# Two Swin blocks in fp16 halves: P transposed by DMA instead of by TensorE

## What is computed

```python
# per block; windows of 8 x 8 points after a shift by 4; 12 heads of 16
xn   = layernorm(x)
q,k,v = split(window(roll(xn)) @ w_qkv + b_qkv)
attn = softmax(q @ k.T * 16**-0.5 (+ rel_bias + shift_mask in the first block))
x    = x + unroll(unwindow((attn @ v) @ w_proj + b_proj))
x    = x + gelu(layernorm(x) @ w_fc1 + b_fc1) @ w_fc2 + b_fc2
```

## Time and profile before

| | before |
|---|---|
| median of 3 runs | 4314.11 us (4303.97 to 4317.73) |
| profiled execution, its span | 4314.22 us, 4312.3 us |
| TensorE matmuls, busy | 4027.5 us, 93% |
| VectorE | 3364.9 us, 78% |
| GpSimd | 3062.7 us, 71% |
| ScalarE | 2709.6 us, 63% |
| packets of the DMA queue, share of 16 engines | 54.9% |
| granted TensorE clock, mean | 0.999 |

### The profile page before, as it was taken

The page is one execution under the profiler, slowest core; times in us unless marked ns, Lnnn a source line. Parts: engine busy times, 40 slices in busy tenths (PEclk is TensorE's granted clock), DMA queues, the critical chain, the costliest instruction groups (busy, mean ns, idle before and its releaser), DMA issues. The chain is left out here.

```text
span 4312.3 us, 175439 instructions
## 1 busy us (share of the span) xinstructions
PE 4027.5 (93%) x66384; PEld 2912.2 (68%) x66384; DVE 3364.9 (78%) x9085; ACT 2709.6 (63%) x5921; POOL 3062.7 (71%) x6257
## 2 busy tenths in 40 slices
PE   4999999999999999999999999999999999999998
PEld 2666667667766666776676677667667766766665
DVE  6887777778778777787777778787777778777785
ACT  1666666666666666666666666666666666666665
POOL 4777777777777777777777777777777777777664
PEclk9999999999999999999999999999999999999999
DMA  4655556556565655555555555556555655565553
GB/s 98 104 96 100 98 95 99 102 95 99 104 98 97 100 102 92 103 100 96 98 100 98 97 99 102 97 97 101 102 91 101 100 97 98 100 101 96 90 95 61
DMA packets 1544449, 420.50 MB, mean 98 GB/s; under 512 B 1441334, under 2 KB 1542074, under 8 KB 1543612
## 3 DMA queue, kind: packets, MB, share of 16 engines
q1 hardware_dynamic: 1543612, 409.29, 54.9%
HBM read 31.56 MB, written 25.17 MB: 13 GB/s over the span
## 5 line engine op out<-in xcount | busy, mean ns | idle before, releaser
L573 PE MATMUL ps_s<-xh,w_fc 128*128 128x512 f16 x3840 | 909.7, 380 | 60.7 <-ACT stage L687 47.6
L941 DVE TENSOR_TENSOR hid<-scaled,hid 128x512 f16<-128x512 f32 x768 | 597.9, 779 | 449.7 <-POOL hid L1109 430.7
L1047 POOL TENSOR_TENSOR rstd<-vare,half 128x2 f32<-128x2 f32 x520 | 361.2, 695 | 801.5 <-DVE vare L881 801.5
L586 PE MATMUL bank<-w_fc,hid 128*128 128x192 f16 x9216 | 847.7, 246 | 77.7 <-DVE hid L941 71.9
L586 PEld LDWEIGHTS bank<-w_fc,hid 128*128 128x128 f16 x9216 | 764.6, 98 | 156.7 <-DVE v_blk L897 80.6
L573 PEld LDWEIGHTS ps_s<-xh,w_fc 128*128 128x128 f16 x3840 | 335.3, 97 | 621.0 <-ACT scaled L701 217.5
L1109 POOL TENSOR_SCALAR hid<-scaled 128x512 f16<-128x512 f32 x768 | 609.4, 794 | 182.8 <-ACT scaled L701 182.2
L701 ACT ACTIVATE scaled<-ps_s,b_fc 128x512 f32<-128x512 f32 x768 | 529.3, 690 | 308.9 <-DVE hid L941 306.8
L693 ACT ACTIVATE pt<-ps_t 128x768 f16<-128x768 f32 x512 | 415.3, 811 | 324.0 <-PE ps_t L530 316.8
L666 ACT ACTIVATE xs<-xn 128x192 f16<-128x192 f32 x512 | 184.6, 361 | 579.0 <-POOL xn L1053 579.0
L449 PE MATMUL bank<-w_qkv,xh 128*128 128x384 f16 x2560 | 500.9, 326 | 6.2 <-DMA xh<-xs 3.6
(11 more groups left out here) (113 smaller groups left out, 7341.9 us busy)
## 6 DMA issues: line engine op xcount, KB each, us to landing
x_img<-in_x_dram SPq DMA_DIRECT2D x256, 96.0 KB, 2.2
out_dram<-y_img SPq DMA_DIRECT2D x256, 96.0 KB, 1.9
xh<-xs SPq DMA_TRANSPOSE x520, 2.8
qkt<-qk SPq DMA_TRANSPOSE x512, 4.0
ot<-os SPq DMA_TRANSPOSE x512, 2.3
stage<-in_L_conv_fc_w_dram SPq DMA_DIRECT2D x2, 384.0 KB, 4.3
stage<-in_L_conv_w_fc_dram SPq DMA_DIRECT2D x2, 384.0 KB, 4.0
stage<-in_L_conv_qkv_w_dram SPq DMA_DIRECT2D x2, 288.0 KB
```

What stands on the lines that cost most here:

```text
L573: last = mm(ps_s[:, u % 2, :].rearrange("p (a t) -> p a t", a=GROUP), w_fc1[layer][:, part, m * 128:(m + 1) * 128], xh[:, p % 2 * GROUP:(p ...
L586: mm(bank[:, 0:C], hid16[:, hs, m, tok], w_fc2[layer][:, ws, m, :], start=(m == 0 and i == 0), stop=False)
L941: v.tensor_tensor(hid16[:, 1, m, :], hid[:, u % 2, :], hid16[:, 0, m, :], ALU.subtract)\
```

## The change

P is not transposed by TensorE any more. ScalarE makes the high half of P straight from `p_tok`, in the slot of the exponential, and VectorE the low half; both halves lie in `p16`, and one DMA transposition of 12 blocks (`p_turn`) brings them into `pt`. The banks `ps_t` become `ps_h` and hold the MLP's hidden products and outputs. `projection` goes into `ps_o` instead of `ps_qk`. The written order changes with it.

```diff
-        ps_t = ctx.enter_context(nc.psum_tensor("ps_t", [128, 2, 512], F32))
+        ps_h = ctx.enter_context(nc.psum_tensor("ps_h", [128, 2, 512], F32))
+        p16 = stage[:, 1, 0:2, :].rearrange("p r n -> p (r n)").bitcast(F16).rearrange("p (r s n) -> p r s n", r=2, s=2)
@@ SyncE
+                def p_turn(n):
+                    ge("p_lo", n)
+                    ge("pv", n - 2)
+                    sp.dma_start_transpose(pt[:, n % 2].rearrange("p s g t -> p (s g) t"),
+                                           p16[:, n % 2].rearrange("p s n -> p (s n)"))\
+                        .then_inc(LANDED["pt_in"][n % 4], 16)
+                if live(s):
+                    p_turn(s)
                 if live(s + 2):
                     qk_turn(s + 2)
@@ TensorE
-                def p_transpose(n):
...
                 def pv_product(n):
-                    if mlp and place == 3:
-                        ge("resid2", p * GROUP + 1)
-                    else:
-                        ge("o_norm", n - 1)
+                    ge("resid1", n - 2)
                     ge("v_lo", n)
-                    ge("p_lo", n)
+                    landed(pe, "pt_in", n)
...
                 def projection(n):
-                    if live(n + 5):
-                        ge("qk_lo", n + 5)
-                    else:
-                        ge("resid1", n - 1)
+                    ge("o_norm", min(n + 1, ENDS))
                     landed(pe, "ot_in", n)
...
                 def hidden(m):
-                        ge("exp_done", min(s, ENDS))
                     if m >= 2:
                         ge("gelu", u - 2)
+                    else:
+                        ge("resid2", (p - 1) * GROUP + 2 + m)
...
                     scores(s)
-                if live(s - 3):
-                    projection(s - 3)
-                if live(s - 1):
-                    p_transpose(s - 1)
+                if live(s + 3):
+                    qk_product(s + 3)
...
                 if live(s):
                     shift_scores(s)
-                if live(s + 3):
-                    qk_product(s + 3)
+                if live(s - 3):
+                    projection(s - 3)
                 if mlp and place == 0:
-                    for m in range(3):
+                    for m in range(4):
                         hidden(m)
@@ ScalarE
                 def p_hi(n):
-                    ge("tp", n)
-                    copy(pt[:, n % 2, 0].rearrange("p (b g) t -> p b (g t)", b=2), ps_t[:, :, 0:3 * TOK], ACT.Copy)\
+                    ge("exp_done", n)
+                    landed(act, "pt_in", n - 2)
+                    copy(p16[:, n % 2, 0], p_tok[:, n % 2].rearrange("p g a k -> p (g a k)"), ACT.Copy)\
...
-                if live(s - 1):
-                    p_hi(s - 1)
                 if live(s):
                     exp(s)
+                    p_hi(s)
@@ VectorE
-                    v.tensor_tensor(pt[:, n % 2, 1].rearrange("p (b g) t -> p b (g t)", b=2), ps_t[:, :, 0:3 * TOK],
-                                    pt[:, n % 2, 0].rearrange("p (b g) t -> p b (g t)", b=2), ALU.subtract)\
+                    v.tensor_tensor(p16[:, n % 2, 1], p_tok[:, n % 2].rearrange("p g a k -> p (g a k)"), p16[:, n % 2, 0],
+                                    ALU.subtract).then_inc(S["p_lo"], 1)
...
-                if mlp and place == 2:
-                    mlp_residual(p * GROUP + 1, ps_o)
                 if live(s + 5) or live(s - 3):
                     centre(s + 5)
-                if live(s - 1):
-                    p_lo(s - 1)
+                if mlp and place == 2:
+                    mlp_residual(p * GROUP + 1)
                 if mlp and place == 0:
                     hidden_lo(0)
+                if live(s):
+                    p_lo(s)
```

More of the change, by code:

```diff
@@ L227, in swin_program @@
             "centred rstd bn1a bn1 ln1 hi1 lo1 qk_mm v_mm mask_set qk_hi qk_lo v_hi v_lo "
-            "s_mm max_done shift exp_done tp p_hi p_lo pv inv_done o_norm o_hi o_lo "
+            "s_mm max_done shift exp_done p_hi p_lo pv inv_done o_norm o_hi o_lo "
             "pr resid1 bn2a bn2 ln2 hi2 lo2 fc2 resid2".split(), TOTAL)
@@ L234, in swin_program @@
         S = {name: sem(name) for name in COUNT}
-        LANDED = {name: [sem(f"{name}{r}") for r in range(4)] for name in ("xh_in", "ot_in", "qkt_in")}
+        LANDED = {name: [sem(f"{name}{r}") for r in range(4)] for name in ("xh_in", "ot_in", "qkt_in", "pt_in")}
         x_loaded = [sem(f"x_loaded{h}") for h in range(2 * SLABS)]
@@ L474, in v_product @@
                     _, layer, t = visit(n)
-                    if place == 1 or p < 0 or p == 0 == place:
-                        ge("v_lo", n - 1)
-                    else:
-                        ge("resid2", p * GROUP + (-1, None, 0, 2)[place])
+                    ge("v_lo", n - 1)
                     for w in range(2):
@@ L490, in rel_scores @@
                     _, layer, t = visit(n)
-                    if place == 1:
-                        ge("gelu", p * HC + HC - 1)
                     ge("exp_done", n - 1)
@@ L576, in hidden, with mlp_out @@
                     last.then_inc(S["fc1"], 1)
-                def mlp_out(n, bank):
+                def mlp_out(n):
                     _, layer, t = visit(n)
+                    bank = ps_h[:, n % 2]
                     tok = slice((t % GROUP) * TOK, (t % GROUP + 1) * TOK)
@@ L605, in slot @@
                     x_transpose(s + 6)
-                if live(s) and place != 1:
+                if live(s):
                     rel_scores(s)
@@ L630, in slot @@
                     shift_scores(s)
-                if live(s + 3):
-                    qk_product(s + 3)
+                if live(s - 3):
+                    projection(s - 3)
                 if mlp and place == 0:
-                    for m in range(3):
+                    for m in range(4):
                         hidden(m)
-                if mlp and place == 2 and visit(p * GROUP)[1] == 1:
-                    y_transpose(p * GROUP + 1)
+                if mlp and place == 2:
+                    mlp_out(p * GROUP + 1)
+                    if visit(p * GROUP)[1] == 1:
+                        y_transpose(p * GROUP + 1)
                 if mlp and place > 0:
-                    ge("v_lo", min(s, ENDS))
-                    if s > ENDS:
-                        ge("resid2", p * GROUP + (0, -1, 0, 2)[place])
-                    mlp_out(p * GROUP + (0, 0, 2, 3)[place], ps_v)
-                if mlp and place == 0:
-                    hidden(3)
+                    mlp_out(p * GROUP + (0, 0, 2, 3)[place])
             tr_reader = ["x_in", -1]
@@ L686, in exp @@
                     ge("shift", n)
+                    ge("p_lo", n - 2)
                     nc.scalar.activation(p_tok[:, n % 2].rearrange("p g a k -> p a g k"),
@@ L980, in slot @@
                 if mlp and place > 0:
-                    mlp_residual(p * GROUP + (0, 0, 2, 3)[place], ps_v)
+                    mlp_residual(p * GROUP + (0, 0, 2, 3)[place])
                 if live(s + 6):
```

38 lines of the change are left out of this document (13 added, 25 removed).

## The result

| | time (median) | ratio to before, 95% interval |
|---|---|---|
| before | 4315.15 us (4303.97 to 4317.73, 4 runs) | 1 |
| changed | 5000.89 us (4982.45 to 5009.01, 4 runs) | 1.1586 (1.1557 to 1.1615) |

The kernel is slower by 686 us. I had forecast 4875 us, 560 us slower, with a range up to 5040.

The account below looks back on a forecast made before the run. VectorE was taken as a second bound beside TensorE, with a VectorE-GpSimd chain in place 0. Places summed to 4.04 us, plus 0.33 for `p_lo`: 4.37 per phase, times 128 is 560, 4314 + 560 = 4874, said 4875; range 4700 to 5040.

Parts of the forecast that it names:

- forecast's own upper end: The highest total of the forecast's own sum, without rivals: 5.1 us per phase, giving 4965 us.
- late transposition: Rival: P's DMA transposition lands after 7.3 us, `pv_product` in place 0 is 1.3 us late, 5040 us; chance 0.10.
- round trip: VectorE's residual waits for row maximum, subtraction on TensorE and projection: 2.04 us against 0.88, 1.16 more per slot.
- Place 0: First slot of a phase: 1.16 us of VectorE waiting plus 0.88 for `p_lo` in the chain, 2.04 us longer.
- Place 1: Second slot of a phase: output product waits for a later last `hidden_lo`; +1.16 and about +0.95 by block, mean +1.05 us.
- TensorE's work behind it is unchanged: +1.16: Place 1, first block: after the first output product's wait TensorE's work stays the same, so the slot grows 1.16 us.
- Places 2 and 3: Last two slots of a phase: place 2 mean -0.05 us without the transposes, place 3 mean +1.0 from VectorE's list.
- y transposition: Place 2, second block: it stands between the two output products and waits for the first one's residual, about +0.2 us.
- `p_lo` from SBUF: VectorE's `p_lo` with both inputs in SBUF: +0.13 us each in two and a half slots, +0.33 per phase.
- The transposition is hidden: P's DMA transposition lands about 9 us behind its row maximum, `pv_product` comes at about +11: hidden by some 2 us.
- below any time considered here: The DMA queue's packets, with 6144 blocks more, take 3540 to 3720 us together, less than any time considered.
- The price of the transposes: TensorE's six transposes per visit take 0.66 us, 338 us in all, gained only where TensorE is waited for.

Follow-up runs that it names:

- Experiment 4: Changed kernel with 24 extra small matmuls on TensorE in place 1, in the wait for the last `hidden_lo`: 4887.4 us, ratio 1.1323.
- experiment 2: Changed kernel with `p_lo` put ahead of the first `hidden_lo` in place 0 again: 4993.7 us, ratio 1.1578.
- experiment 5: Both orders put back in the changed kernel, plus the projection back in `ps_qk` with TensorE's order and waits of before: 4502.7 us, ratio 1.0435.
- experiment 7: The kernel before with P's six TensorE transposes done twice: 4531.75 us, ratio 1.0506.
- Experiments 1: Changed kernel with the projection ahead of `qk_product` and the subtraction of the maximum again on TensorE, still into `ps_o`: 4838.9 us, ratio 1.1208.
- 3: Changed kernel with both the projection's order on TensorE and `p_lo`'s order in place 0 put back: 4718.1 us, ratio 1.0943.
- 8: The kernel before with one more, unread DMA transposition of 12 blocks per visit, issued ahead of `qk_turn`: 4370.7 us, ratio 1.0137.
- 12: Experiment 5 with only P's high half transposed (6 blocks instead of 12) from the third visit on: 4437.6 us, ratio 1.0284.
- 9: Experiment 5 with `qk_turn` issued behind `o_turn` in SyncE's list: 4845.5 us, ratio 1.1233.

## Why the prediction was right, and what it missed

The direction, the mechanism and nearly all slot lengths came out as forecast; the time lies 126 us above the forecast. It is also above the forecast's own upper end of 4965. That the stated range holds it is luck: its upper end, 5040, was the time of the late transposition, a rival that did not happen. The forecast's own range was also added up too narrowly: a round trip of 1.0 to 1.3 us counted in three places, with `p_lo` at 0 to 1.1, gives 3.6 to 5.6 us per phase, some 4770 to 5030 us, and not 3.8 to 5.1.

In mean slot lengths the profiled run (4982 us) grew by 2.47, 1.96, -0.07 and 0.85 us in places 0 to 3, 5.21 us per phase. The sum had 2.04, 1.05, -0.05 and 1.0, and 0.33 for `p_lo`, 4.37 us; 0.84 x 128 is the 107 us by which this run is over the forecast.

- *The round trip.* Forecast 2.04 us against 0.88, in every slot; the trace has 2.04, 2.03 (2447.82 less 2445.79) and 2.09 (2456.81 less 2454.72), in 512 slots, 588 us of waiting against "some 500". Right.
- *Place 0.* Forecast 14.6; median 14.68, mean 15.0. The second `hidden_lo` is 2.36 us later, forecast 2.04. The median is right, but of the 2.36 only 2.04 was priced; the rest is the first `hidden_lo`, 1.02 us long instead of 0.69. The mean is 0.3 us higher for another reason that I had no term for: in 26 of 126 phases the granted clock falls to 0.50 in this place, and these are 16.2 us long on average, the others 14.7.
- *Place 1: the term that was mis-sized.* "TensorE's work behind it is unchanged: +1.16" holds in block 1, 6.81 to 7.92, +1.11. In block 2, where I forecast +0.95, the median went from 6.32 to 8.90, +2.58. The wait before the output product rose to 2.2 us as forecast, but I priced the work behind it at its old duration. In 51 of 62 phases of block 2, and in 22 of 64 of block 1, the granted clock halves after this wait, and 18 matmuls take 3.06 us instead of 1.66. Experiment 4 isolates it: 113 us. In means place 1 grew by 1.96 us instead of 1.05, and 0.91 x 128 is 116 us. The other misses nearly cancel: place 0 took 0.43 us more, place 3 took 0.15 less, and the 0.33 for `p_lo` did not come.
- *Places 2 and 3.* Forecast 7.4 and 6.9. Mean of both blocks 7.58 and 6.8. Right within 0.2; the second block's extra (8.01 against 7.13) is larger than the 0.2 that I gave the y transposition.
- *`p_lo` from SBUF.* Forecast +0.13 us each; it takes 950 ns against 956 before:

```profile
L890 DVE TENSOR_TENSOR stage<-stage 128x768 f16<-128x768 f32 x512 | 486.4, 950 | 6.2 <-ACT stage L676 5.4
```

  The 0.33 us of this term came elsewhere, in the first `hidden_lo` (0.69 to 1.02 us), which now runs beside GpSimd's second `hidden_hi`. That the sum has the right amount there is luck. Beside `p_lo` it is GpSimd that pays, `rstd` 695 to 972 ns:

```profile
L1028 POOL TENSOR_TENSOR rstd<-vare,half 128x2 f32<-128x2 f32 x520 | 505.5, 972 | 1214.3 <-DVE vare L863 1214.3
```

```profile
2450.26 0.95 DVE L890 TENSOR_TENSOR stage<-stage 128x768 f16<-128x768 f32 x1
...
2450.49 1.27 POOL L1028 TENSOR_TENSOR rstd<-vare,half 128x2 f32<-128x2 f32 x1 [3.27 <-DVE vare L863]
...
2458.89 0.70 POOL L1028 TENSOR_TENSOR rstd<-vare,half 128x2 f32<-128x2 f32 x1 [2.48 <-DVE vare L863]
```

  The first `rstd` began 0.23 us into a `p_lo` and took 1.27 us. The second began 0.16 us ahead of the next `p_lo` (2459.05) and took 0.70. The Trainium skill (SBUF — State Buffer, section "SBUF: two separate sides") says that of a VectorE instruction with two SBUF inputs and a GpSimd one that reads SBUF, the one that starts first gets the shared ports for the whole instruction and the other is blocked. The first `rstd` agrees with it in direction. The second pair does not: this `p_lo` began 0.54 us ahead of `rstd`'s end and still took 0.95 us. In the changed kernel `rstd` of place 0 ends ahead of `p_lo` and keeps 0.69 us; it is long in places 1 and 3, where VectorE hardly ever waits for GpSimd. What it costs on the chain shows in experiment 2.
- *The transposition is hidden.* It lands after 3.5 us, and `pv_product` waits 1.3 us for it in the whole run. Right, for the changed kernel, whose places 1 and 3 are 0.85 to 2 us longer than before. But "below any time considered here" was an average, and slot by slot there was no room even here. Places 2 and 3 of the changed kernel, with their shares of 0.89 and 1.03:

```profile
2417.19:2424.34 7.15, 7.15 (x137) 5.93 (x136) 5.65 (x18) 4.07 (x11) 4.95 (x12) 1.00 0.89 140
2424.34:2431.12 6.78, 5.84 (x119) 4.58 (x118) 5.29 (x16) 3.00 (x7) 3.98 (x8) 1.00 1.03 146
```

  Little waits for what is late there, but not nothing:

```profile
PE bank L460 <- DMA xh<-xs: 68.7, 66, 3.6
```

  These are `qk_product`'s waits for the norms, 3.6 us before. 49 of them are in place 3. Twelve are in place 0, 1.9 us each, and the longest of these are in the phases in which the granted clock falls early in the place. In experiment 5, with TensorE's order of before, it is the projection that waits, for `o`'s transposition.
- *The price of the transposes.* Forecast at most 338 us and only where TensorE is waited for; experiment 7 puts six more at 218. TensorE's share, forecast at 75% or so, is 79%.

What my account had wrong beyond the sum is that it read as though the round trip caused the loss and its removal would end it. Experiments 1 and 3, which took the order back, came out 500 us above their expectations. Behind the round trip stood, in this order as the edits uncovered them: the projection's bank with TensorE's order around it (215 us, experiment 5); the exponential, `p_hi` and `p_lo` in one slot (232 us of waits of `p_lo` for `p_hi` left in 5; no run prices them); the full queue (57 us in 8, 65 us in 12). Back from the changed kernel, order and place bring 283 us and the bank with its order 215. The 188 us that are left sit in place 0: summed over the phases it is 229 us longer than before in kernel 5, and the other three places together are 41 us shorter. With `ot` in time (9) 71 of the 229 are left, though 9 also changes the other places. Two rivals for the rest were not taken apart by a run: the granted clock, which falls in place 0 in 53 of 126 phases of kernel 5, and making both halves of P in the exponential's own slot.

## What to carry to other kernels

Take the slot lengths from the trace and price each new wait; then ask a second time what the engine does right after a wait that has grown to 2 us, since its next work may run at half the clock. A chain whose removal is forecast to give back X gives back only what the next chain allows: where an edit moves a bank, an order and a transfer at once, undo all of them, and each alone where you can, before saying which was the cause. Read the share of the DMA engines slot by slot, not as an average.

## What was not expected of the hardware

- TensorE's granted clock fell to 0.50 for 18 matmuls after 2.20 us of standing (3.06 against 1.66 us), and did not in another phase after the same 2.20 us; 24 unneeded matmuls in the gap made the kernel 113 us faster.
- A VectorE subtraction with both inputs in SBUF keeps its 950 ns and stretches a GpSimd instruction of two columns that starts behind it from 0.70 to 1.27 us, in kernel 5 to 1.48. Another VectorE subtraction, of 128x512, that starts while GpSimd's `hidden_hi` runs is itself stretched, from 0.69 to 1.02 us.
- DMA transpositions of 12 blocks of 128x128 fp16 land in 3.5 to 4.3 us; with 12 unread blocks more per slot the `qkt` one took 4.9. The engines' share reached 1.02 in a slot of 7 us of kernel 5, at 156 GB/s.
